# A scan kernel's first border: inputs loaded before it, rates stored at another place, one product moved

## What is computed

```python
XQ, XK, XV = heads(xn @ q_w.T), heads(xn @ k_w.T), heads(xn @ v_w.T)     # 32 heads of 16, chunks of 16 tokens
eta = token_idx * sigmoid(xn @ ttt_lr_weight.T + ttt_lr_bias) / 16       # learning rates
for each chunk (32, one after the other; W1_s, b1_s carried):
    Z1 = xk @ W1_s + b1_s
    grad = ln_fused_l2_bwd(Z1, xv - xk, ln_w, ln_b)
    out = xq + ln(xq @ W1_s - eta * tril(xq @ xk.T) @ grad + b1_s - tril(eta) @ grad)
    W1_s, b1_s = W1_s - (eta[-1] * xk).T @ grad, b1_s - sum(eta[-1] * grad)
attn = ln(out) @ o_w.T
ffn  = (silu(xn @ gate_w.T * gate_s) * (xn @ up_w.T * up_s)) @ down_w.T * down_s   # 1408 wide
x = x + attn + ffn
```

## Time and profile before

| | us |
|---|---|
| median of 3 runs | 2028.1 (2024.35 to 2031.59) |
| the profiled execution | 2030.79 |
| its span in the profile | 2029.1 |
| TensorE busy in the span | 1888.4 (93%) |
| last matmul of stage one starts | 191.65 |
| first feed-forward matmul starts | 205.80 |

### The profile page before, as it was taken

How to read it: one execution, slowest core, us unless ns; L and a number is a source line. 1 busy time by engine, 2 the same in 40 slices (tenths; PEclk the granted TensorE clock), 3 DMA queues, 4 the chain that set the end, 5 groups by cost and what they waited for, 6 DMA issues and landing times. The chain is left out here.

```text
span 2029.1 us, 34768 instructions
## 1 busy us (share of the span) xinstructions
PE 1888.4 (93%) x12632; PEld 1425.2 (70%) x12632; DVE 1213.4 (60%) x2400; ACT 979.8 (48%) x2117; POOL 1031.0 (51%) x904
## 2 busy tenths in 40 slices
PE   5898899998989999889899989999999999999998
PEld 3676777665666665577787867777777777777776
DVE  4562566677786774457335446666666666666663
ACT  3332556555565655544434426444444444444442
POOL 5444567556565654420134337555555555555552
PEclk9898999999999999979999999999999999999999
DMA  7785657335333633241678871232233223222321
GB/s 241 272 304 185 222 164 270 110 115 206 115 113 110 213 107 103 63 137 58 223 244 268 275 261 42 94 115 94 91 127 115 85 83 131 109 76 79 111 98 43
DMA packets 157112, 297.97 MB, mean 147 GB/s; under 512 B 20240, under 2 KB 97296, under 8 KB 150288
## 3 DMA queue, kind: packets, MB, share of 16 engines
q1 hardware_dynamic: 155856, 294.70, 43.0%
q10 hardware_dynamic: 1088, 1.05, 0.2%
HBM read 221.52 MB, written 74.19 MB: 146 GB/s over the span
## 5 line engine op out<-in xcount | busy, mean ns | idle before, releaser
L1979 POOL TENSOR_SCALAR probs<-probs,rsum 128x512 f32<-128x512 f32 x256 | 396.5, 1568 | 246.3 <-DVE rsum L2115 246.3
L2079 ACT ACTIVATE p_tok<-bank 128x512 fp32r<-128x512 f32 x256 | 154.9, 608 | 343.5 <-PE bank L2019 343.4
L2111 DVE TENSOR_REDUCE nmax<-bank 128x1 f32<-128x512 f32 x256 | 158.9, 683 | 95.1 <-PE bank L2011 95.1
L2121 DVE TENSOR_TENSOR p_tok<-bank,p_tok 128x512 fp32r<-128x512 f32 x256 | 173.3, 679 | 15.9 <-ACT p_tok L2079 15.8
L2071 ACT ACTIVATE probs<-bank,nmax 128x512 f32<-128x512 f32 x256 | 173.0, 693 | 3.3 <-DVE nmax L2111 3.3
L60 PE MATMUL bank<-xs,ffn_w 128*128 128x512 f32 x352 | 153.0, 435 | 13.9 <-issue 9.2
L1467 POOL TENSOR_TENSOR y_pieces<-y_tok,y_pieces 128x512 fp32r<-128x512 f32 x48 | 65.5, 1379 | 184.6 <-ACT y_pieces L1672 184.5
L2019 PE MATMUL bank<-ident,probs 128*128 128x128 f32 x1024 | 156.1, 276 | 2.8 <-DVE p_tok L2121 2.8
L2019 PEld LDWEIGHTS bank<-ident,probs 128*128 128x128 f32 x1024 | 121.9, 140 | 50.8 <-issue 27.2
L1101 DVE SCALAR_TENSOR_TENSOR pt<-bank,t_mask 128x256 f32<-128x256 f32 x256 | 91.7, 413 | 92.7 <-PE bank L883 91.3
L61 PE MATMUL bank<-xs,ffn_w 128*128 128x512 f32 x352 | 138.8, 394 | 0.0
(11 more groups left out here) (277 smaller groups left out, 4971.4 us busy)
## 6 DMA issues: line engine op xcount, KB each, us to landing
ffn_w<-ffn_pieces SPq DMA_DIRECT2D x120, 512.0 KB, 3.7
uvo<-uvo_pieces SPq DMA_DIRECT2D x15, 2048.0 KB, 8.8
wq<-wq_pieces SPq DMA_DIRECT2D x16, 1536.0 KB, 6.4
ffn_pieces<-stage SPq DMA_DIRECT2D x30, 512.0 KB, 4.1
xs<-xn_pieces SPq DMA_DIRECT2D x4, 2048.0 KB, 7.9
y_tok<-in_gup SPq DMA_DIRECT2D x32, 256.0 KB, 3.6
wk<-wk_pieces SPq DMA_DIRECT2D x16, 512.0 KB, 3.7
ffn_w<-ffn_pieces SPq DMA_DIRECT2D x16, 384.0 KB, 3.4
```

Source lines behind the costliest of these rows:

```text
L1979: nc.gpsimd.tensor_scalar(probs[:, u % 8, :], probs[:, u % 8, :], rsum[:, u % 8:u % 8 + 1], None, ALU.mult).then_inc(norm_done, 1)
L2079: nc.scalar.activation(p_tok[:, Q % 2, 0, :, hh * P:(hh + 1) * P], banks[4 + u % 2][:].rearrange("p (k q) -> p k q", k=NBLK), ACT.Copy).th ...
L2111: nc.vector.tensor_reduce(nmax[:, u % 8:u % 8 + 1], banks[u % HG][:], axis=X_AXIS, op=ALU.max, negate=True).then_inc(max_done, 1)
L2121: nc.vector.tensor_tensor(p_tok[:, Q % 2, 1, :, q], banks[4 + u % 2][:].rearrange("p (k q) -> p k q", k=NBLK), p_tok[:, Q % 2, 0, :, q].bi ...
```

## The change

- `xs` and `ffn_w` get fixed addresses at the start of stage one's region, so that they exist before the border. The six weight tiles are put in another order: `xs` lies on K's two tiles (`kw_hi`, `kw_lo`), the first four slots of `ffn_w` on V's (`kvw_hi`, `kvw_lo`), the fifth slot on Q's. Stage two only reserves the room (`home_of_xs_and_fw`).
- SyncE loads the first `xs` in block 3 behind the stores of slot 0, once K's products of block 3 are done.
- ScalarE's queue loads the first four weight pieces, behind its `cst` stores, once V's products of block 3 are done.
- `move_rates` is split: one transfer instead of four stores the rates, ahead of the piece stores of slot 1; the eight loads stay at the end. VectorE's factor 1/16 moves from behind V's four evictions to behind the second.
- TensorE does the first product of the feed-forward (four trips, twelve matmuls) before `turn_k(0)`; the first step's share has four trips less.

```diff
@@ -135,11 +135,15 @@
         ff_sc = s0("ffn_scales", [P, 2, NI])
         hd = lambda ap: ap.rearrange("p (x d) -> p x d", d=HD)
         over_d = lambda ap: ap.unsqueeze(2).broadcast_to([P, NX, HD])
+        NWP, NEARLY = 5, 4
+        xs_in, fw_in = sem("ttt_xs_in"), [sem(f"ttt_fw_in{i}") for i in range(NWP)]
 
         with ExitStack() as st:
             s = sb_in(st)
-            kw_h, qw_h, vw_h = [s(n + "_hi", [P, NF, HID], F32R) for n in ("kw", "qw", "kvw")]
-            kw_l, qw_l, vw_l = [s(n + "_lo", [P, NF, HID], F32R) for n in ("kw", "qw", "kvw")]
+            first_home = (nc.sbuf_base + 31) // 32 * 32
+            kw_h, kw_l, vw_h, vw_l, qw_h, qw_l = [s(n, [P, NF, HID], F32R) for n in ("kw_hi", "kw_lo", "kvw_hi", "kvw_lo", "qw_hi", "qw_lo")]
+            xs = nc.alloc_sbuf_tensor_at("xs", [P, 2, NF, TB], F32R, offset=first_home)
+            fw = nc.alloc_sbuf_tensor_at("ffn_w", [P, NWP, 2, NF, P], F32R, offset=first_home + 16 * 1024)
             x_sb, xc = s("x_sb", [P, NF, TB]), s("xc", [P, NF, TB])
             xs_hi, xs_lo = s("xs_hi", [P, NF, TB], F32R), s("xs_lo", [P, NF, TB], F32R)
             sq, x_sum, v_sum, std = s("sq", [P, 2, TB]), s("x_sum", [P, TB]), s("v_sum", [P, TB]), s("std", [P, TB])
@@ -248,30 +252,40 @@
                                 sp.dma_start(cst_dram[8 * m:8 * m + 8, t, e, :, :],
                                              cs[:, q % NCS, e * HX:(e + 1) * HX]).then_inc(cst_out[q % NCS], 16)
 
-                    def move_rates():
+                    def store_rates():
                         sp.wait_ge(sig_done, 2)
-                        for b in range(BATCH):
-                            sp.dma_start(lr_dram[b].rearrange("(m n) t e x -> (n t) m (e x)", m=NF), lr_raw[:, NF * b:NF * b + NF, :]).then_inc(lr_out, 16)
-                        sp.wait_ge(lr_out, 16 * BATCH)
+                        sp.dma_start(lr_dram.rearrange("b (m n) t e x -> (n t) (b m) (e x)", m=NF), lr_raw[:]).then_inc(lr_out, 16)
+
+                    def load_rates():
+                        sp.wait_ge(lr_out, 16)
                         for b in range(BATCH):
                             for e in range(2):
                                 c = 32 * b + 16 * e
                                 sp.dma_start(lr[c:c + 16, :, :], lr_dram[b].rearrange("n t e x -> t e n x")[:, e, :, :]).then_inc(lr_in, 16)
+
+                    def load_first_xs():
+                        sp.wait_ge(job_ready, JT * (NTB - 1) + NF)
+                        sp.wait_ge(xs_out, 32)
+                        sp.dma_start(xs[:].bitcast(F32), xs_pc[0]).then_inc(xs_in, 16)
 
                     for t in range(NTB):
                         sp.wait_ge(lo_done, NF * (t + 1))
                         sp.dma_start(xs_pc[t][:, 0, :, :], xs_hi[:].bitcast(F32)).then_inc(xs_out, 16)
                         sp.dma_start(xs_pc[t][:, 1, :, :], xs_lo[:].bitcast(F32)).then_inc(xs_out, 16)
                         for slot in range(3):
+                            if t == NTB - 1 and slot == 1:
+                                store_rates()
                             for i in split_at(t, slot):
                                 store_piece(i)
                                 for r in raw_of[i]:
                                     load_raw(r + NRAW)
+                            if t == NTB - 1 and slot == 0:
+                                load_first_xs()
                             if slot == 1 and t + 2 < NTB:
                                 load_x(t + 2)
                         if t < NTB - 1:
                             store_cst(t)
-                    move_rates()
+                    load_rates()
                     sp.wait_ge(xs_out, 32 * NTB)
                     for i in range(NST):
                         sp.wait_ge(st_out[i], 16 * len(range(i, NPC, NST)))
@@ -445,6 +459,11 @@
                         for e in range(2):
                             act.dma_start(cst_dram[8 * m:8 * m + 8, NTB - 1, e, :, :],
                                           cs[:, q % NCS, e * HX:(e + 1) * HX]).then_inc(cst_out[q % NCS], 16)
+                    act.wait_ge(job_ready, JT * (NTB - 1) + 2 * NF)
+                    for w in range(NEARLY):
+                        act.wait_ge(st_out[w % NST], 16 * (w // NST + 1))
+                        n = width(JOBS_T[w])
+                        act.dma_start(fw[:, w, :, 0:n, :].bitcast(F32), fw_pc[w][:, :, 0:n, :]).then_inc(fw_in[w], 16)
 
                 @block.vector
                 def _(dve):
@@ -546,20 +565,19 @@
                                     if q >= NCS:
                                         dve.wait_ge(cst_out[q % NCS], 32 * (q // NCS))
                                     nc.vector.tensor_tensor(cs[:, q % NCS, :], b_row[:], banks[J % 4][:], ALU.add).then_inc(ev_dve, 1)
+                                    if t == NTB - 1 and j == 1:
+                                        dve.wait_ge(sig_done, 1)
+                                        nc.vector.tensor_scalar_mul(lr_raw[:], lr_raw[:], 1.0 / HD).then_inc(sig_done, 1)
                             if kind == kinds(t)[1] and t + 1 < NTB:
                                 normalize(t + 1)
-                            if kind == kinds(t)[1] and t == NTB - 1:
-                                dve.wait_ge(sig_done, 1)
-                                nc.vector.tensor_scalar_mul(lr_raw[:], lr_raw[:], 1.0 / HD).then_inc(sig_done, 1)
                         if t == 0:
                             scan_constants()
 
 
         with ExitStack() as st:
             s = sb_in(st)
-            NWP, LAG = 5, 9
-            xs = s("xs", [P, 2, NF, TB], F32R)
-            fw = s("ffn_w", [P, NWP, 2, NF, P], F32R)
+            LAG = 9
+            s("home_of_xs_and_fw", [P, 36 * 256])
             hid_hi, hid_lo = s("hid_hi", [P, 4, TB], F32R), s("hid_lo", [P, 4, TB], F32R)
             silu_g, up_sb, hid, dn_sb = [s(n, [P, 2, TB]) for n in ("silu_g", "up_sb", "hid", "down_sb")]
             acc = s("ff_acc", [P, NF, TB])
...
@@ -660,10 +677,8 @@
                             sp.wait_ge(acc_out, 16 * NF * t)
                         sp.dma_start(acc[:], fm(A["xT"])[:, :, t * TB:(t + 1) * TB]).then_inc(acc_in, 16)
 
-                    load_xs(0)
-                    load_fw(0)
                     load_cst(0)
-                    for j in range(1, NWP):
+                    for j in range(NEARLY, NWP):
                         load_fw(j)
                     load_cst(1)
                     load_acc(0)
...
                 def _(pe):
                     def ffn(n, i):
                         for x in range(*seg(n, i)):
-                            j, k = TRIPS[x]
...
+                            if x >= NF:
+                                trip(x)
+
+                    def trip(x):
+                        j, k = TRIPS[x]
...
+                        if k == 0:
+                            pe.wait_ge(fw_in[j % NWP], 16 * (j // NWP + 1))
+                            if j >= 2:
+                                pe.wait_ge(ev_sem[kind_of(j - 2)], nth(j - 2) + 1)
+                            if kind == "gate":
+                                pe.wait_ge(xs_in, 16 * (t + 1))
...
+                        ins = exact_matmul(nc, bank[:], wh, wl, xh_, xl_, start=(k == 0), stop=(k == w - 1))
+                        if k == w - 1:
+                            ins.then_inc(f_ready, 1)
...
+                    for x in range(NF):
+                        trip(x)
                     turn_k(0)
                     for n in range(END):
```

More of the change, by code:

```diff
@@ L591, in build @@
                      "oxh_done oy_done oq_done chain zero_done f_ready ev_gate ev_up ev_down prod_done hhi_done hlo_done acc_done "
-                     "grad_in xs_in acc_in acc_out")
+                     "grad_in acc_in acc_out")
             (w_done, z_ready, sq_done, var_done, std_done, sg_done, sgbd_dve, sgbd_act, ssum_done, d_done, wx_dve, wx_act, snap_done, sz_done, wsx_done,
@@ L595, in build @@
              oxh_done, oy_done, oq_done, own, zero_done, f_ready, ev_gate, ev_up, ev_down, prod_done, hhi_done, hlo_done, acc_done,
-             grad_in, xs_in, acc_in, acc_out) = [sem("ttt_" + x) for x in names.split()]
+             grad_in, acc_in, acc_out) = [sem("ttt_" + x) for x in names.split()]
             wx_zero = sem("ttt_wx_zero")
@@ L599, in build @@
             grad_out = [sem("ttt_grad_out0"), sem("ttt_grad_out1")]
-            fw_in = [sem(f"ttt_fw_in{i}") for i in range(NWP)]
             NPART = NSUPER * NF * BATCH
@@ L822, in ffn @@
-                            if kind == "down" and o < 2:
-                                pe.wait_ge(hlo_done, NI * t + THIRDS[a][0] + k + 1)
-                            wh, wl = fw[:, j % NWP, 0, k, :], fw[:, j % NWP, 1, k, :]
-                            if kind == "down":
-                                xh_, xl_ = hid_hi[:, k, :], hid_lo[:, k, :]
-                            else:
```

(23 more changed lines are left out.)

## The result

| | before | changed |
|---|---|---|
| median of 20 runs each, us | 2028.28 | 2033.62 |
| ratio, with its 95% interval | | 1.0026 (1.0017 to 1.0035) |
| profiled execution, span | 2030.79, 2029.1 | 2029.81, 2027.9 |
| VectorE's last copy of q starts | 192.08 | 190.28 |
| first issue behind the border | 196.40 | 204.95 |

What follows compares the result with a forecast made beforehand. TensorE, busy 93%, bounds the kernel, so only its waits and half-clock stretches count. Border +3.0 and behind it -4.2 give -1.2 on the profiled 2030.8: 2029.6; the median, 2.7 lower, 2026.9; 8-in-10 range 2019.5 to 2032.

Steps and rivals of the forecast that it cites:

- The border: End of stage one's barrier, SyncE's first issue behind it at 196.4: forecast to come 3.0 us later, waiting for the rates.
- their issue keeps its 6.5 us: SyncE's eight loads of the learning rates before the barrier: issuing them was to take 6.5 us as before.
- The start of the loads: SyncE's rates loads: to begin at 187.5 give or take 1, the store ahead of them landing behind xs.
- wait for the store: Sign on SyncE before the rates loads: its wait for the rates' store would end at 187 to 189.
- The far end: Latest barrier end: +5.6, from 4.8 us of added transfers that don't fit idle time and up to 0.8 later start.
- Behind the border: From the barrier to the second step's state product: 20.4 us instead of 24.6, a gain of 4.2, range 2.8 to 5.5.
- The state update: First step behind the barrier: could start at +15.15 instead of +20.7, before losses to GpSimd's product and TensorE's clock.
- the loss to GpSimd's product: First step's VectorE chain: the product of gate and up slows small VectorE instructions, costing 0 to 1.0 us.
- a clock lost in TensorE's gap: TensorE before the first state update: a new gap of 1.8 to 2.8 us may cost 0 to 1.7 us.
- Rival 2: Early loads become the barrier's wait, +5.6 or more, only 2.8 comes back in the first step: 2030.9 to 2034; chance 0.16.
- Rival 1: Rates get through before the barrier, VectorE's last copy of q sets it: -3.2, with -4.2 together -7.4, 2020.7; chance 0.22.
- ScalarE's weight issues: ScalarE issuing four weight pieces behind its cst stores: 1.4 to 3.3 us, hidden under SyncE's wait.

Runs made afterwards that it cites:

- e2: Changed kernel with xs loaded by SyncE behind the border and the first product behind the state product again, weights still early: 2025.2 us, one run.
- e3: Changed kernel with rates scaled and stored earlier, loaded behind slot 0's piece stores, and xs loaded behind slot 1's: 2028.2 us, ratio 1.0005.
- e7: Kernel before with only the change's rates part (one earlier store, VectorE's factor moved), nothing loaded early: 2025.1 us, ratio 0.9989.
- e9: e7 with, behind the border, the first weight piece loaded ahead of xs, and xs by four loads, one per trip: 2025.8 us, ratio 0.9987.
- e10: e2 with xs loaded behind the border by four loads, one for each trip of the first product: 2022.7 us, ratio 0.9968.
- e8: Changed kernel with the rates' store put ahead of the xs load on SyncE's queue: 2032.7 us, one run.
- e1: Changed kernel with all five weight pieces loaded by SyncE behind the border instead of four by ScalarE ahead of it: 2029.5 us, ratio 1.0012.
- e5: Rates first as in e3, xs loaded once K's products are done, only the first weight piece early, on SyncE's queue: 2027.5 us, ratio 0.9996.
- e6: e3 with the xs load cut into eight loads with rows of 2 KB instead of 16 KB: 2032.0 us, one run.

## Why the prediction was wrong, point by point

- **The border: this is the step that failed.** The direction was right, the size was not: +3.0, with 5.6 as the far end, against +10.4 measured. The sentence that failed is "their issue keeps its 6.5 us". The issue of the eight loads took 15.8 us; that is 9.2 of the 10.4, and the later start is the other 1.1. The prediction took the issue for fixed and charged only bytes that don't fit. The runs show that the issuing engine itself is held: 4.6 to 6.5 us for these loads with no large load in flight (before, e2, e3, e7, e9, e10), 15.8 with the weights, 17.6 with xs and the weights (e8).
- **The start of the loads came when I had said, in part for another reason.** The store did land behind xs (9.9 us). But SyncE shows no wait for the store, which I had named as a sign. It was held in the issue of the first piece store, for 6.9 us. To the three piece stores between store and loads I had given no time at all. No run parts the two.
- **The far end was wrong as a bound.** It added engine time: 10.1 us of new transfers less 5.3 us of idle. That holds only if the engines stay full until the end. They did up to 199 (busy share 1.01 from 183 on); then the share was 0.49 from 199 to 202, and 0.38 from 202 to 204, with 1152 rows in 2 us. Because the rates were held back, their issue was too, and at the end it ran alone with the engines half idle. Time given to the large transfers first isn't made up behind them. My own row had pointed that way: from 190 to 193 the rates moved at 573 rows per us beside cst, at over 900 alone. It gave the direction and not the size, for it has no 4 KB rows in it.
- **Behind the border: the number was right, by two errors that cancel.** Forecast were 20.4 us and a gain of 4.2, measured 20.3 and 4.2. The state update came at +16.5, 0.8 later than the 15.65 in my middle (15.15 and half of GpSimd's 1.0): all twelve matmuls of the head start ran at half clock, 0.43 us apart, 5.2 us instead of 4.4, and Square stood at +8.1 instead of +7.55. Two of VectorE's small instructions took 0.36 and 0.66 us (L1143, L1144) instead of 0.18 each, which fits the loss to GpSimd's product that I had put at 0 to 1.0. On the other side, the 0.85 us for a clock lost in TensorE's gap did not come: the gap stood as two, 1.44 and 0.78, and the matmuls behind each were soon 0.23 apart again. In e8, with the same program behind the border, the matmuls stood 0.43 us apart up to the eighth and 0.23 behind it; the twelve took 4.4 us, and S was 19.6. So 0.7 us of S hangs on when the clock rises (TensorE in e8):

```profile
206.26 0.55 PE L61 MATMUL bank<-xs,ffn_w 128*128 128x512 f32 x1
206.65 0.40 PE L62 MATMUL bank<-xs,ffn_w 128*128 128x512 f32 x1
206.89 0.39 PE L60 MATMUL bank<-xs,ffn_w 128*128 128x512 f32 x1
...
207.57 0.60 PE L885 MATMUL bank<-ident,kz 128*128 128x128 f32 x4
```

- **Rival 2 happened in its first half.** The early loads became the border's wait, at 10.4 where it said 5.6 or more. Its second half did not happen: it had only 2.8 us come back in the first step, and 4.2 did. Its time, 2030.9 to 2034, holds the measured one, in part by luck. I gave it 0.16, and cut the range at 2032.
- The Trainium skill (DMA: Bandwidth & Descriptors, Queues, rings and completion order) stood beside the term with two rules: each DMA engine takes turns between queues packet by packet, and a semaphore increment lands behind all earlier writes of that engine. The trace agrees with the first in kind: both queues moved where both had work, two short rows for each long one here and about four for one before; what makes up a packet no run shows. It agrees with the second on one queue, with 9.9 us to landing for the store behind xs; no run shows it across queues.
- **Rival 1** (the rates get through) is refuted for the change, and true of e2 and e7, where nothing stands ahead.
- VectorE's scaling, ScalarE's weight issues (5.04 us instead of 1.4 to 3.3, still under SyncE's wait) and the buffer waits cost nothing at the end, as said.

## What to carry to other kernels

A prefetch ahead of a barrier is not free because the DMA engines have idle time there: look at what the barrier itself waits for, and whether that is a chain of small transfers, since these are what a large one beside them holds up here. Put the small chain first and let it land, then issue the large loads: the same 2 MB of weights cost nothing where the rates' loads were issued before them (e2), and 6.6 us where they weren't (the changed kernel against e1). Then look for the next small chain: in e3 and e5 the cst stores took the rates' place as the border's wait.

## What the runs showed of the hardware that I had not expected

- Eight loads of 32 KB each (rows of 64 bytes) took 4.7 us to issue with no large load in flight (e2), 6.5 in the kernel before, 8.8 behind xs (e1), 15.8 beside weights, 17.6 beside xs and weights (e8). A single store of 384 KB behind xs and the rates' store was held 6.9 us. So the issuing engine is held, not only the data.
- Short-row throughput beside 2 MB of loads on the other queue fell from over 900 to 198 rows per us; 1 KB stores fell to 159 rows in 6 us beside xs (e3).
- Cutting the large transfer's rows from 16 to 2 KB let 0.56 MB instead of 0.15 pass on the other queue in 6 us, and gave only 0.6 us of D's 9.1 (e6, one run).
